# One visit instead of two: the second product of the triangular inverse's 16 level on TensorE

## What is computed

```python
q = silu(_causal_dwconv(x @ Wq, qcw, qcb))      # k, v the same way
...
def step(S, inps):
    qt, kt, vt, at, bt = inps
    Sk = jnp.einsum('bhvk,bhk->bhv', S, kt)
    err = Sk - vt
    S = at[..., None, None] * S - bt[..., None, None] * (err[..., None] * kt[:, :, None, :])
    ot = jnp.einsum('bhvk,bhk->bhv', S, qt)
    return (S, ot)
```

## Time and profile before

| what | value |
|---|---|
| device time, median of 3 runs | 3139.67 us |
| span of the profiled execution, first to last instruction | 3137.5 us |
| the difference, around the span | 2.2 us |
| TensorE matmuls busy | 3080.8 us, 98% |
| TensorE weight loads busy | 2546.7 us, 81% |
| VectorE busy | 2028.1 us, 65% |
| ScalarE busy | 1658.5 us, 53% |
| GpSimd busy | 1306.9 us, 42% |
| matmuls / weight loads | 23992 / 23992 |
| first and last start of the visits' matmuls (line 958) | 442.1 and 1788.9 us |

### The profile page before, as it was taken

One profiled execution on the slowest core, in us unless ns is written; L12 is line 12 of the kernel. 1 busy time (PEld: TensorE's weight loads), 2 busy tenths in 40 slices (PEclk: granted clock), 3 DMA queues, 4 the chain that ended last, 5 costly groups with the idle time before them and its releaser, 6 DMA issues. The chain is left out here.

```text
span 3137.5 us, 61518 instructions
## 1 busy us (share of the span) xinstructions
PE 3080.8 (98%) x23992; PEld 2546.7 (81%) x23992; DVE 2028.1 (65%) x3590; ACT 1658.5 (53%) x3882; POOL 1306.9 (42%) x2223
## 2 busy tenths in 40 slices
PE   8999989999999999999999899999999999999999
PEld 7888868888888888888888778778888888888887
DVE  6112268778877878777878543656666666666666
ACT  5221357777778777777777643344333333222222
POOL 2222235655556555565655434313333322222212
PEclk9999999999999999999999899999999999999999
DMA  2100111111111111111111154411010110000004
GB/s 92 31 21 28 69 55 42 46 55 52 51 42 47 55 55 55 44 43 55 52 49 45 49 178 138 124 38 31 27 31 27 45 33 31 24 21 27 24 17 161
DMA packets 130243, 165.70 MB, mean 53 GB/s; under 512 B 9936, under 2 KB 72144, under 8 KB 129920
## 3 DMA queue, kind: packets, MB, share of 16 engines
q1 hardware_dynamic: 120592, 144.49, 15.2%
q10 hardware_dynamic: 9296, 17.04, 1.5%
q0 software_dynamic: 64, 0.23, 0.0%
HBM read 127.91 MB, written 33.82 MB: 52 GB/s over the span
## 5 line engine op out<-in xcount | busy, mean ns | idle before, releaser
L1444 DVE SCALAR_TENSOR_TENSOR b_zt<-b_rx,b_cw,b_zt 128x512 f32<-128x512 f32 x576 | 461.7, 802 | 21.6 <-POOL b_rx L1643 3.1
L70 PE MATMUL bank<-b_XH,b_wh 128*128 128x512 f32 x1024 | 462.6, 452 | 9.7 <-ACT b_zt L1200 8.9
L72 PE MATMUL bank<-b_XH,b_wl 128*128 128x512 f32 x1024 | 403.9, 394 | 0.0
L71 PE MATMUL bank<-b_XL,b_wh 128*128 128x512 f32 x1024 | 402.8, 393 | 0.2 <-issue 0.2
L70 PE MATMUL bank<-b_XH,b_qh 128*128 128x512 f32 x1024 | 399.0, 390 | 1.6 <-DVE b_g L2586 1.4
L72 PE MATMUL bank<-b_XH,b_ql 128*128 128x512 f32 x1024 | 398.4, 389 | 0.0
L71 PE MATMUL bank<-b_XL,b_qh 128*128 128x512 f32 x1024 | 398.4, 389 | 0.0
L2696 POOL TENSOR_TENSOR b_QHL<-b_qhd,b_QHH 128x512 fp32r<-128x512 f32 x124 | 176.6, 1428 | 453.1 <-ACT b_QHH L2464 450.8
L1688 POOL TENSOR_TENSOR b_PR<-b_A,b_T 128x15 f32<-128x15 f32 (+7 forms) x480 | 169.9, 354 | 166.3 <-issue 132.0
L2464 ACT CAST b_QHH<-b_qhd 128x512 fp32r<-128x512 f32 x124 | 76.9, 623 | 293.8 <-PE bank L72 176.8
L72 PEld LDWEIGHTS bank<-b_XH,b_wl 128*128 128x128 f32 x1024 | 192.9, 188 | 44.4
(11 more groups left out here) (259 smaller groups left out, 7649.9 us busy)
## 6 DMA issues: line engine op xcount, KB each, us to landing
b_abc<-tmp_a SPq DMA_DIRECT2D x64, 256.0 KB, 3.5
b_gbc<-tmp_g SPq DMA_DIRECT2D x64, 256.0 KB, 3.8
tmp_og<-b_gg SPq DMA_DIRECT2D x64, 256.0 KB, 2.4
b_mo<-tmp_og SPq DMA_DIRECT2D x64, 256.0 KB, 3.1
b_wr<-in_Wk SPq DMA_DIRECT2D x16, 256.0 KB, 3.1
b_wr<-in_Wq SPq DMA_DIRECT2D x16, 256.0 KB, 4.4
b_wr<-in_Wv SPq DMA_DIRECT2D x16, 256.0 KB, 2.7
b_wr<-in_Wg SPq DMA_DIRECT2D x16, 256.0 KB, 4.2
```

The costliest lines, as they stand in the source:

```text
L70: e.do.matmul(out, wh, xh, start=first and k == 0, stop=False)
L71: e.do.matmul(out, wh, xl, start=False, stop=False)
L72: m = e.do.matmul(out, wl, xh, start=False, stop=last and k == n - 1)
L1444: e.do.scalar_tensor_tensor(out=z[:, :], in0=rx[:, j:j + 512], scalar=cw[:, u // 2, KIND[name[0]], j:j + 1], in1=z[:, :], op0=ALU.mult, op ...
```

## The change

`inverse4` loses its bounds and does all 8 matrices in one call, at the place where its first half stood. Its waits are the same, and they stand ahead of the first matmul as before; the semaphore `s4` is raised by its last matmul. The steps k1 3-4 and q1 2-3 of the projections now come behind all 128 small matmuls, not behind 64 of them.

```diff
-    def inverse4(u, m0, m1):
+    def inverse4(u):
...
-        if m0 == 0:
-            bank_free(e, "s4a", u)
-            e.wait_ge("zs", u + 1)
-        for m in range(m0, m1):
+        bank_free(e, "s4a", u)
+        e.wait_ge("zs", u + 1)
+        for m in range(8):
...
-        if m1 == 8:
-            r.then_inc(S["s4"], 1)
+        r.then_inc(S["s4"], 1)
...
         inverse3(i - 1)
         project(i, "q1", 1, 2)
-        inverse4(i - 1, 0, 4)
+        inverse4(i - 1)
         project(i, "k1", 3, 4)
         project(i, "q1", 2, 3)
-        inverse4(i - 1, 4, 8)
         project(i, "q1", 3, 4)
         project(i, "v1", 0, 1)
         inverse5(i - 1)
```

## The result

The changed kernel takes 3154.83 us (median of 5 runs, 3151.3 to 3157.63); the kernel before took 3139.58 in the same series (3137.38 to 3140.08). The ratio is 1.0049, 95% interval 1.0039 to 1.0060: slower by 0.5%. The forecast was 3153.5.

A forecast was written before the change was run, and what follows sets the result against it. TensorE's own list of work was taken as the bound. Span 3137.5 us, -5.8 for the saved switch less v1's wait, +20.0 for instruction pauses, +2.2 around the span gave 3153.9, rounded to 3153.5; range 3147 to 3160.

The forecast's parts named there:

- Term 1: At inverse4's two visits on TensorE: merging removes one switch to small matmuls, -0.31 us in 31 rounds, -9.7 us.
- Term 2: At v1's first matmul: a new wait for ScalarE to empty k1's bank cuts the net saving to -0.19 us a round.
- Term 3: Around the merged visit, TensorE pauses at ends of 256-instruction blocks: 23.7 us instead of 3.7, +20.0 us.
- Rival (a): At block ends: instruction supply keeps up, so no new pauses; 3133.9 us, or 3130.0 without v1's wait; 13%.
- Rival (b): In the merged visit: supply is worse, instructions enter slower or 17 pauses last 2.5 us each; 3172 us; 8%.
- Rival (c): At the merged visit and v1: pauses come but v1's wait does not; 3150.0 us, counted in the forecast's 79%.

The follow-up runs named there:

- e1: Changed kernel with projection step k1 3-4 moved ahead of the merged inverse4 visit; 3138.77 us, ratio 0.9994 to the kernel before.
- e2: Changed kernel with the merged inverse4 visit two steps later, behind k1 3-4 and q1 2-3; 3129.88 us, ratio 0.9968 to the kernel before.
- e3: Changed kernel with only 4 of the 8 matrices in inverse4, so 64 matmuls a visit; 3118.77 us, ratio 0.9933 to the kernel before.
- e4: Changed kernel with 16 more transposes at TensorE's start, moving later instructions 32 places in their 256-blocks; 3159.99 us, ratio 1.0061 to the kernel before.
- e5: Changed kernel with the merged inverse4 visit three steps later, behind q1 3-4 and ahead of v1; 3132.02 us, ratio 0.9977 to the kernel before.

## Why the prediction was right

**Term 1** (switch saved, -0.31 us a round) had the right cause and was a little small: with no wait behind it the round is 0.36 us shorter (e1, e2). The reason is in the visit itself: 128 matmuls start within 1.10 us, not in twice 0.57. Most of it is in the second 64, which take 0.54 us, the 8.4 ns that I had kept as a bound.

**Term 2** (v1's wait) is right: 1.99 us from k1's last matmul to v1's second, as read off round 0. It takes 0.14 us a round back (-0.36 to -0.22). The two together were put at -0.19 a round, -5.8 us, and are -0.22, -6.8 us, the other end of what the prediction allowed for the pace. (31 times 0.19 and 0.31 are 5.9 and 9.6; the prediction's 5.8 and 9.7 are a tenth off, which changes nothing.) e1 shows the pair from the other side: with k1 ahead of the visit, the wait goes.

**Term 3** (instruction blocks) carried the sign. Forecast: 23.7 us of pauses instead of 3.7. Measured: 22.7 instead of 3.8. The 22.7 of the table leaves out unit 30's pause (1.5) and takes in the halved clock (1.4); the two cancel, and the 17 pauses by themselves sum to 22.7 as well. The 2.56 us from a packet's start to the next instruction were 2.2 to 2.9. The largest errors are single units, and they cancel: by the prediction's rule unit 17 comes to about 1.2 us and has 2.0, because its packet started 0.7 us behind the visit's start and not ahead of it; unit 8 comes to about 1.3 and has 0.9. That the places came out one by one is no luck; that the sum is right to 1 us is partly that.

**What the forecast did not have** is the halved clock, 1.4 us. It is the one place where a pause cost more than its own length.

**The sum.** -6.8 + 22.7 - 3.8 + 1.4 = +13.5 us from the visits and the clock; the profile shows +15.4 and the medians +15.2. Of the 1.9 us that are left, 1.2 lie ahead of the first visit, where the first projection starts at 392.7 us before and at 393.9 after with the same instructions; over all eight profiles that start scatters from 392.4 to 394.9. Of the other 0.7, 0.4 lie behind unit 31's visit. They are in the scatter of the runs, which is 6 us wide for the changed kernel, and were not traced. So the 3153.5 is near 3154.8 in part by chance: what the forecast left out (the clock and the later start, 2.6 us) is about made up by pauses put 1 us too high and a saving put 1 us too low.

**Rival (a)**, the supply that keeps up, falls with e2, e3 and e4. The rule of the Trainium skill that it leaned on ("Runtime: NRT & Kernel Launch", "Instruction fetch mechanics": a block crossing is mostly hidden) holds for the rest of this kernel: in the changed one some 105 of 122 block ends in rounds 2 to 31 cost nothing. It fails at the 17 ends where the packet had started too late: it started 0.3 to 1.8 us behind the first instruction of the block before, and 2.2 to 2.9 us more passed until the next block began, while those blocks take only 1.3 to 2.7 us without their pauses. **Rival (b)** fails too: beside their pauses the visits of units 1 to 30 run at 8.6 to 8.9 ns a matmul, no slower than before, and the 17 pauses sum to some 22.7 us, 1.3 us each and not 2.5. **Rival (c)** is excluded: v1's wait is there also in rounds that pause inside the visit, 27 times and 8.4 us in all between 480 and 1750 us.

Two things stay open. One is what makes a packet start late. The prediction's reading, that a block is asked for only when the one before it has been entered, is too simple if "entered" means TensorE's first start in it. At the pauses of the changed kernel the packet started 0.3 to 1.8 us behind that start. But elsewhere between 480 and 1750 us it started up to 3.5 us ahead of it, and in e5 1.4 us ahead, which is why 1.5 us for a block cost nothing there. What all eight profiles agree on is the block's end: over all packets, the next block never begins less than 2.16 us behind its packet's start. The runs give the rule for the end of a block, not for the request. The other is which pause is followed by the halved clock: it isn't the length alone, since 1.4 us idle was followed by it in e1, and 1.9 us was not in e4.

## What to carry to other kernels

Merging two short visits of small matmuls saves a switch (0.36 us here), but look at what the merged run does to the instruction stream: here 256 instructions in 1.1 us, with 128 more 1 us ahead, outran the supply and cost some three times what the merge saved (6.8 us with v1's wait). Put large instructions that are there anyway between such runs: here the 256 instructions up to a point of the visit took 2.1 us in the changed kernel and 3.5 in e2, where few pauses are left, and the same merge two steps later made the kernel 0.3% faster than before (e2). An idle time "<-issue" that returns every multiple of 256 instructions is the sign to look for.

## What the runs showed of the hardware that I had not expected

- Matmuls of 32x32, each with its own weight load, start 8.6 ns apart over a run of 128 at full clock (1.10 us); no visit of units 1 to 30 ran slower than 8.9 ns except at a block's end.
- The idle time of 0.36 us before the weight load of `inverse5` is put down to VectorE in e5 and to nothing in the changed kernel, and its length is the same, while the wait of a weight load ahead of a large one (v1, 0.3 us) cost 0.14 us. The idle time in such a row, and the name beside it, are not the loss.
- Behind a pause of 1.4 to 2.1 us the granted clock can be 0.50 for 3.4 us: once in the changed kernel, once in e1 and once in e4, at 1.3 to 1.5 us each. Most pauses of that length weren't followed by it.
- Shortening TensorE's round by 0.75 us (e3) was enough for VectorE's masks to become the later one in every second round, though VectorE is busy only 65% of the span.
